# First attention's prologue: bf16 parts taken off in PSUM, rotary in halves, values projected last

## The reference

```python
qkv = jnp.einsum('bnc,dc->bnd', x, W_qkv)
qkv = qkv.reshape(B, N, 6, H, hd).transpose(2, 0, 3, 1, 4)      # H = 16 heads, hd = 8
q = jnp.concatenate((qkv[0], qkv[1]), axis=-1)
k = jnp.concatenate((qkv[2], qkv[3]), axis=-1)
v = jnp.concatenate((qkv[4], qkv[5]), axis=-1)
q = q * cos + rotate_half(q) * sin
k = k * cos + rotate_half(k) * sin
attn1 = jnp.einsum('bhid,bhjd->bhij', q1, k1) * scale
attn2 = jnp.einsum('bhid,bhjd->bhij', q2, k2) * scale
probs = softmax(attn1) - lam * softmax(attn2)
out = einsum('bhij,bhjd->bhid', probs, v)                       # then W_proj
```

## Time and profile before

| | us |
|---|---|
| median of 3 runs | 522.52 |
| lowest and highest | 520.49, 528.23 |
| the profiled execution | 522.95 |
| its span (first to last instruction) | 521.1 |
| PE busy in it | 462.1 (89%) |
| DVE busy in it | 283.0 (54%) |
| DVE's first rotary product to PE's first scores of head 0 | 9.92 to 38.18 |

### The profile page before, as it was taken

One profiled execution on the slowest core, in us unless ns is written; L12 is line 12 of the kernel. 1 busy time (PEld: TensorE's weight loads), 2 busy tenths in 40 slices (PEclk: granted clock), 3 DMA queues, 4 the chain that ended last, 5 costly groups with the idle time before them and its releaser, 6 DMA issues.

```text
span 521.1 us, 10953 instructions
## 1 busy us (share of the span) xinstructions
PE 462.1 (89%) x4143; PEld 333.5 (64%) x4144; DVE 283.0 (54%) x690; ACT 224.5 (43%) x402; POOL 119.1 (23%) x231
## 2 busy tenths in 40 slices
PE   9568999988679998899999597998898999999993
PEld 3424777755445984356767366877795577777773
DVE  2945678724782537554624588988324333332326
ACT  1541677662131424314564246766604543333440
POOL 4821454432300112212211253352200000000001
PEclk9978999999959999989999789999999999999997
DMA  7666454232300001563111000200000011101111
GB/s 179 218 220 150 142 156 153 71 110 86 129 34 1 1 3 32 155 162 103 42 30 40 11 11 18 52 1 0 3 2 11 22 40 40 40 29 32 40 32 41
DMA packets 23020, 34.41 MB, mean 66 GB/s; under 512 B 7568, under 2 KB 15712, under 8 KB 22720
## 3 DMA queue, kind: packets, MB, share of 16 engines
q1 hardware_dynamic: 22976, 33.81, 22.0%
HBM read 28.26 MB, written 5.24 MB: 64 GB/s over the span
## 4 chain that ended last, share of the span: by engine, by line
PE 57%; issue 13%; DVE 12%; DMA 7%; POOL 5%; SPq 2%; ACT 2%; POOLq 0%; DVEq 0%; ACTq 0%
PE ps L1024 11%; PE ps L1007 11%; PE ps L642 4%; PE ps L620 4%; POOL probs L575 4%; PE ps L607 4%; PE ps L995 3%; PE ps L596 2%; PE ps L830 2%; PE ps L864 2%; PE ps L654 2%; DVE arena L1431 2%; DVE arena L1417 2%; DVE bst L1391 2%; PE ps L604 2%
## 5 line engine op out<-in xcount | busy, mean ns | idle before, releaser
L1348 DVE TENSOR_REDUCE negm<-ps 128x4 f32<-128x512 f32 x96 | 64.1, 688 | 43.1 <-PE ps L607 42.0
L1671 DVE SCALAR_TENSOR_TENSOR racc<-ps,sm,racc 128x128 f32<-128x128 f32 x128 | 35.9, 343 | 63.2 <-PE ps L1024 63.1
L1072 ACT ACTIVATE arena<-ps,w1a 128x512 f32<-128x512 f32 x64 | 43.4, 687 | 59.0 <-PE ps L1007 57.8
L1072 ACT ACTIVATE probs<-ps 128x512 f32<-128x512 f32 (+1 forms) x100 | 56.4, 593 | 24.5 <-PE ps L620 23.4
L1024 PEld LDWEIGHTS ps<-w1a,arena 128*128 128x128 f32 x512 | 59.4, 192 | 7.2 <-issue 6.2
L1024 PE MATMUL ps<-w1a,arena 128*128 128x128 f32 x512 | 59.8, 275 | 0.8 <-DVE racc L1662 0.8
L1007 PE MATMUL ps<-xT,w1a 128*128 128x512 f32 x128 | 58.0, 594 | 1.4 <-ACT xT L1072 1.4
L596 PE MATMUL ps<-onesb 128*128 128x512 bf16 x150 | 44.7, 434 | 9.3 <-ACT vall L1072 6.2
L531 POOL TENSOR_SCALAR rstd<-mv 128x4 f32<-128x4 f32 x12 | 2.7, 227 | 182.8 <-DVE mv L1394 182.8
L575 POOL TENSOR_TENSOR probs<-probs,rzE 128x480 f32<-128x480 f32 x32 | 30.6, 987 | 51.7 <-DVE rzE L1613 51.7
L1072 ACT ACTIVATE arena<-ps 128x512 f32<-128x512 f32 (+3 forms) x47 | 26.3, 573 | 32.8 <-PE ps L830 15.4
(11 more groups left out here) (207 smaller groups left out, 826.4 us busy)
## 6 DMA issues: line engine op xcount, KB each, us to landing
stackA<-arena SPq DMA_DIRECT2D x12, 256.0 KB, 2.8
arena<-stackA SPq DMA_DIRECT2D x24, 96.0 KB
arena<-stackA SPq DMA_DIRECT2D x8, 288.0 KB
w1a<-in_w1a SPq DMA_DIRECT2D x1, 2048.0 KB, 8.4
w2a<-in_w2a SPq DMA_DIRECT2D x1, 2048.0 KB, 7.7
w1a<-in_w1b SPq DMA_DIRECT2D x16, 128.0 KB, 2.0
w1a<-in_w2b SPq DMA_DIRECT2D x16, 128.0 KB, 2.0
stackD<-arena SPq DMA_DIRECT2D x6, 256.0 KB
```

Source lines behind the costliest of these rows:

```text
L1072: return nc.scalar.activation(o, i, f, **kw)
L1348: nc.vector.tensor_reduce(negm[:, slot % 2, 4 * g:4 * g + 4], tiles(bank(BANK_S + g % 2), 4, P), AX.X, ALU.max, negate=True).then_inc(a.ma ...
L1671: last = stt(racc[:, b, :], bank(banks + half)[:, k * P:(k + 1) * P], sm[:, 11, bass.ds(b * E1 + e, 1)], racc[:, b, :], ALU.mult, ALU.add)
```

## The change

Only the prologue of the first attention is changed, and the order of the loads.

- DVE's rotary works in four turns: (queries, first half of the tokens), (queries, second half), (keys, first half), (keys, second half). A turn is four products of 512 columns from PSUM into `rope`, a wait for them, and two sums of 512 columns, which DVE now makes itself and **writes back into the two PSUM banks** the operands came from (`A.full`). POOL's four sums are gone.
- ACT rounds from PSUM (512 columns) to part 0. PE then **subtracts** it in PSUM: a bf16 matmul of 512 columns with a stationary minus identity (`minusb`), accumulating on what lies in the bank (`take_off`). ACT rounds the rest to part 1, PE takes it off, ACT rounds to part 2. So DVE's eight instructions of the split are gone, ACT has 24 of 512 columns in place of 8 of 1024, and PE has 16 more matmuls.
- PE makes the projections in the order of the turns; the values come behind the last `take_off`, then the context's keys and values behind `A.lo` 8, and 10 dummy matmuls in place of 26.
- `con` is loaded in three DMAs in place of one: the queries' tables third in the order, ahead of the second half of `xT`; the identity; the rest. `xT`'s first half goes ahead of `wqk0`. `ld_x` now counts `wv0` too.
- SP keeps the parts of n = 0 and 1 when their second half is done, then those of n = 2 and 3, in the order part 0, 1, 2.

```diff
+            load(xT[:, 0:HALF], d["xT"][:, 0:HALF], ld_a)
             load(wqk0[:], d["wqk0"], ld_a)
-            load(xT[:, 0:HALF], d["xT"][:, 0:HALF], ld_a)
+            load(con[:, C_COSQ:C_COSK], d["con"][:, C_COSQ:C_COSK], ld_t)
             load(xT[:, HALF:T], d["xT"][:, HALF:T], ld_h)
-            load(con[:, 0:C_IOTA], d["con"][:, 0:C_IOTA], ld_c)
-            load(wv0[:], d["wv0"], ld_b)
+            load(con[:, 0:C_COSQ], d["con"][:, 0:C_COSQ], ld_c)
+            load(con[:, C_COSK:C_IOTA], d["con"][:, C_COSK:C_IOTA], ld_c)
+            load(wv0[:], d["wv0"], ld_x)
...
-                sp.wait_ge((a.hi, a.mid, a.lo)[p], n + 1)
+                sp.wait_ge((a.hi, a.mid, a.lo)[p], n + 1 if a is D else n // 2 * 4 + n % 2 + 3)
...
-            for n, p in ((0, 0), (1, 0), (0, 1), (2, 0), (1, 1), (0, 2), (3, 0), (2, 1), (1, 2), (3, 1), (2, 2), (3, 2)):
+            for n, p in ((2 * k + m, p) for k in range(2) for p in range(PARTS) for m in range(2)):
...
-            for n in range(4):
-                pool.wait_ge(A.mul, n + 1)
-                op = ALU.subtract if n % 2 == 0 else ALU.add
-                nc.gpsimd.tensor_tensor(rope[:, 2 * n, :], rope[:, 2 * n, :], rope[:, 2 * n + 1, :], op).then_inc(A.full, 1)
-            pool.wait_ge(A.lo, 4)
+            pool.wait_ge(A.full, 8)
             nc.gpsimd.memset(ones_deep, ONES_PAIR).then_inc(zeros, 1)
...
+            def take_off(p, turn):
+                side, half = divmod(turn, 2)
+                for m in range(2):
+                    n = 2 * side + m
+                    pe.wait_ge((A.hi, A.mid)[p], 2 * turn + m + 1)
+                    mm(bank(2 * n + half), minusb[:], part[:, n, p, half * HALF:(half + 1) * HALF],
+                       start=False, stop=True, skip_group_check=True).then_inc((A.rest, A.rest2)[p], 1)
...
+            pe.wait_ge(tables, 5)
+            for turn in range(4):
+                take_off(0, turn)
+                take_off(1, turn)
+            pe.wait_ge(ld_x, 16 * 8)
+            pe.wait_ge(A.lo, 4)
+            first_values(0)
+            first_values(1)
+            first_values(2)
+            first_values(3)
+            pe.wait_ge(A.lo, 8)
...
-            keep_busy(26, BANK_M0)
+            keep_busy(10, BANK_M0)
...
+            for turn in range(4):
+                side, half = divmod(turn, 2)
+                for p, ready, made in ((0, A.full, A.hi), (1, A.rest, A.mid), (2, A.rest2, A.lo)):
+                    for m in range(2):
+                        n = 2 * side + m
+                        act.wait_ge(ready, 2 * turn + m + 1)
+                        fn(part[:, n, p, half * HALF:(half + 1) * HALF], bank(2 * n + half), ACT.Copy).then_inc(made, 1)
...
+            def rotary(side, half):
+                cos, sin = ((C_COSQ, C_SINQ), (C_COSK, C_SINK))[side]
+                dve.wait_ge(A.qk, 2 * side + half + 1)
+                first, second = 2 * side, 2 * side + 1
+                cols = slice(half * HALF, (half + 1) * HALF)
+                for n, other in ((first, second), (second, first)):
+                    for k, (t, table) in enumerate(((n, cos), (other, sin))):
+                        dch(tt(rope[:, 2 * n + k, cols].rearrange("p (a b) -> p a b", b=P),
+                               tiles(bank(2 * t + half), 4, P), over(con[:, table:table + P], 4), ALU.mult))
+                dch.wait()
+                for n, op in ((first, ALU.subtract), (second, ALU.add)):
+                    tt(bank(2 * n + half), rope[:, 2 * n, cols], rope[:, 2 * n + 1, cols], op).then_inc(A.full, 1)
...
-            rotate(0)
-            rotate(1)
-            rotate(2)
-            rest_part(A, 0)
-            rotate(3)
-            rest_part(A, 1)
-            low_part(A, 0)
-            rest_part(A, 2)
-            low_part(A, 1)
-            rest_part(A, 3)
-            low_part(A, 2)
-            low_part(A, 3)
+            dve.wait_ge(ld_t, 16)
+            rotary(0, 0)
+            rotary(0, 1)
+            dve.wait_ge(ld_c, 32)
+            rotary(1, 0)
+            rotary(1, 1)
```

More of the change, by code:

```diff
@@ L116, in decoder_kernel @@
         con = sb("con", [P, C_ALL])
-        identb, trib, onesb, causS, causT = (sb(n, [P, P], BF16) for n in ("identb", "trib", "onesb", "causS", "causT"))
+        identb, trib, onesb, causS, causT, minusb = (
+            sb(n, [P, P], BF16) for n in ("identb", "trib", "onesb", "causS", "causT", "minusb"))
         one = sb("one", [P, 1])
@@ L250, in along @@
             return ap.unsqueeze(2).to_broadcast([ap.shape[0], ap.shape[1], n])
-        ld_a, ld_h, ld_b, ld_c, ld_l, ld_x, ld_r, ld_f, ld_d = (sem(f"ld_{n}") for n in "ahbclxrfd")
+        ld_a, ld_h, ld_c, ld_l, ld_x, ld_r, ld_f, ld_d = (sem(f"ld_{n}") for n in "ahclxrfd")
         zeros = sem("zeros")
@@ L256, in decoder_kernel @@
         tables = sem("tables")
+        ld_t = sem("ld_t")
         dchain, achain, pchain = sem("dchain"), sem("achain"), sem("pchain")
@@ L265, in __init__ @@
                 self.qk = sem(n + "_qk")
-                self.mul = sem(n + "_mul") if turns == 0 else None
+                self.rest2 = sem(n + "_rest2") if turns == 0 else None
                 self.full = sem(n + "_full")
@@ L543, in _ @@
             rsqrt(0, 1)
-            pool.wait_ge(ld_x, 16 * 7)
+            pool.wait_ge(ld_x, 16 * 8)
             add_bias(1, bvB)
@@ L746, in _, with first_values @@
             pe.wait_ge(ld_a, 32)
-            for t in range(4):
+            for side in range(2):
                 for half in range(2):
-                    if t == 0 and half == 1:
+                    if half == 1 and side == 0:
                         pe.wait_ge(ld_h, 16)
[L751 to L756, removed]
+                    for t in (2 * side, 2 * side + 1):
+                        last = mm(bank(2 * t + half), wqk0[:, t, :], xT[:, half * HALF:(half + 1) * HALF],
+                                  start=True, stop=True)
+                    last.then_inc(A.qk, 1)
+            def take_off(p, turn):
[5 more added lines that the diff above has]
+                       start=False, stop=True, skip_group_check=True).then_inc((A.rest, A.rest2)[p], 1)
+            def first_values(g):
                 for k in range(2):
@@ L760, in _ @@
                 last.then_inc(A.vps, 1)
-            pe.wait_ge(ld_x, 16 * 7)
-            pe.wait_ge(A.mul, 4)
+            pe.wait_ge(tables, 5)
[9 more added lines that the diff above has]
+            pe.wait_ge(A.lo, 8)
             for half in range(2):
@@ L773, in _ @@
             pe.wait_ge(fixed, 8)
-            keep_busy(26, BANK_M0)
+            keep_busy(10, BANK_M0)
             pe.wait_ge(bkvc, 4)
             pe.wait_ge(fixed, 8)
-            pe.wait_ge(tables, 4)
             heads(A, NH, pair=False, causal=False)
@@ L1140, in table_of @@
                 ach.wait()
-            act.wait_ge(ld_c, 16)
+            act.wait_ge(ld_c, 32)
+            fn(minusb[:], ident, ACT.Copy, scale=-1.0).then_inc(tables, 1)
             for dst, c in ((identb, C_ID), (trib, C_TRI), (causS, C_CS), (causT, C_CT)):
@@ L1148, in values @@
                 fn(vall[:, 2 * g:2 * g + 2, :], bank(g).rearrange("p (a b) -> p a b", a=2), ACT.Copy).then_inc(A.vall, 1)
-            part_hi(A, 0, rope[:, 0, :])
-            part_hi(A, 1, rope[:, 2, :])
-            part_mid(A, 0, rope[:, 1, :])
+            for turn in range(4):
[5 more added lines that the diff above has]
+                        fn(part[:, n, p, half * HALF:(half + 1) * HALF], bank(2 * n + half), ACT.Copy).then_inc(made, 1)
             values(0)
             values(1)
[L1155 to L1159, removed]
             values(2)
@@ L1431, in low_part @@
                 tt(part[:, n, 2, :], rope[:, 2 * n + 1, :], part[:, n, 1, :], ALU.subtract).then_inc(a.lo, 1)
-            def rotate(n):
-                dve.wait_ge(A.qk, 2 if n < 2 else 4)
-                rotary(n, 0 if n < 2 else 4, *((C_COSQ, C_SINQ) if n < 2 else (C_COSK, C_SINK)))
-            rotate(0)
-            rotate(1)
-            rotate(2)
-            rest_part(A, 0)
-            rotate(3)
-            rest_part(A, 1)
-            low_part(A, 0)
-            rest_part(A, 2)
-            low_part(A, 1)
-            rest_part(A, 3)
-            low_part(A, 2)
-            low_part(A, 3)
+            dve.wait_ge(ld_t, 16)
[4 more added lines that the diff above has]
+            rotary(1, 1)
             dve.wait_ge(ld_l, 16 * 6)
```

## The result

| | us |
|---|---|
| changed kernel, median of 20 runs | 520.94 (518.83 to 527.01) |
| kernel before, median of 20 runs | 524.67 (520.49 to 542.69) |
| ratio | 0.994, interval 0.9917 to 0.9963 |
| the profiled execution of the changed kernel, and its span | 521.54, 519.4 |

The changed kernel is faster by 0.6%, some 3.1 us (1.9 to 4.4), less than the 2% that count as a change here. The ratio leaves out the executions that ran at a lower granted clock, so it isn't the quotient of the two medians. The forecast of 517.6 was a gain of 4.9 on 522.52, the median of three runs of the kernel before. Twenty give 524.67. So of the 3.3 us between forecast and result, 2.15 are this start, and about 1.2 (4.9 less 524.67 - 520.94 = 3.7) the gain itself.

A forecast was written before the change was run, and what follows sets the result against it. It took DVE's rotary and split, then write landings and head stacks, to bound the prologue. 3.65 + 1.25 = 4.9 us off 522.95 gave 518.05, less 0.4 to the median: 517.6, range 514 to 521.8.

The forecast's parts named there:

- DVE bounds the prologue, and the split's subtractions are what to take off it: Prologue: DVE on the chain without a gap from 9.92 to 30.64 us, the split's last subtraction at 28.29.
- DVE starts at 7.7; a turn is 3.75; last sum at 22.8: Rotary on DVE: start after two projection matmuls instead of four, then four turns of products and sums.
- The sums' price, 0.60 apart: DVE's sums into PSUM, which no row priced: 0.60 us taken, 1.7 as upper bound; each 0.1 more costs 0.8.
- DVE paces, ACT has slack: Rotary turns: ACT needs 3.0 to 3.5 us a turn, less than DVE's 3.75.
- Last part at 25.8, writes landed at 28.5, 4.3 us earlier: End of the split: last rounding at 25.8 instead of 30.64, plus 2.1 and 0.6 for the writes to land.
- The queue of writes: Last parts' writes: six of 256 KB released within 3 us, so 0.6 us added to the landing.
- PE's values at 25.3, at half clock until 28.8; heads from 36.4: PE behind the last subtraction: values until 30.7, context's projections until 34.3, 10 dummies, then heads; head 2 reached at 42.5.
- The thin stretch: PE during the turns: 16 matmuls of 0.2 to 0.4 us in 12 us, which should bring the half clock.
- The dip behind this wait: Half clock behind PE's wait for head 2's stack, expected to go with the 1.9 us stall, worth 1.25 us.
- 3.65 + 1.25 = 4.9 at head 1: Heads: PE reaches head 2 at 42.5 instead of 46.15, 3.65 us earlier, and the vanished half clock gives 1.25.
- Nothing behind that is changed: Rest of the kernel: code unchanged, so the whole 4.9 us comes off the profiled 522.95, giving 518.05.
- The rival "more": No half clock at 25, no queued writes, 6.3 us gained: 516.3; later dips may differ by a us or two; chance 0.15.

The follow-up runs named there:

- five profiles: Profiles with the old prologue's DVE work: kernel before, its repeat, twice with 40 more dummy matmuls, once with new load order; stack loads issued at 31.53 to 32.82 us.
- the second pair: Kernel before and changed kernel, both run again unchanged: ratios 1.0002 and 0.9897 to the kernel before, spans 522.7 and 516.9 us.
- the second profile: The changed kernel run again unchanged: ratio 0.9897 to the kernel before, span 516.9 us, head 1 at 47.95.
- The first pair: First profiles of the kernel before and the changed kernel: spans 521.1 and 519.4 us; ratio 0.994.
- The four comparisons: Changed kernel against kernel before: first run, repeat, and both kernels with 40 more dummy matmuls, twice; 3.1, 5.4, 5.0 and 4.3 us faster.
- the nine profiles of the table: Kernel before twice, with new loads, with sums on DVE; changed twice, with 26 dummies, values earlier, DVE held; 467.6 to 471.2 us behind head 1.
- the 40 dummies: 40 more dummy matmuls in PE's waits behind the first attention: ratios 0.9943, 0.9944 on the kernel before; 0.9847, 0.9862 on the changed kernel.

## Why the prediction was right or wrong

- *DVE bounds the prologue, and the split's subtractions are what to take off it.* The first half is shown: the stack loads followed DVE's first product by 22.9 us in five profiles, and the sums alone on DVE made head 1 4.2 us later. Of the 4.8 us at the stack loads some 2.4 came with the subtractions, the sums and the halves together, and the rest goes with the earlier start; what the subtractions alone are worth isn't shown.
- *DVE starts at 7.7; a turn is 3.75; last sum at 22.8.* It started at 7.20, a turn was 3.72 (7.20, 10.93, 14.65, 18.37), the last sum ended at 22.18. Right. Starts differ by over a microsecond from run to run in both kernels, which I had not allowed for.
- *The sums' price, 0.60 apart.* 0.696 us long, 0.60 apart. Right. The 120 cycles against 58 of the Trainium skill (VectorE: DVE Perf Modes, "The TRN2 errata") are for results in SBUF, and the difference isn't seen here either: the sums, which read SBUF (and write PSUM), took 15 ns more than the products, which read PSUM, and not some 65 less, as an estimate from these two figures would have it.
- *DVE paces, ACT has slack.* Only half right. The chain lies on ACT and PE from 12.2 on. ACT's last turn took 3.6 us (eight roundings without a gap in 4.81), where 3.0 to 3.5 was expected, so nothing is left below a start of 7.5.
- *Last part at 25.8, writes landed at 28.5, 4.3 us earlier.* 25.41 and 27.97, 4.8 earlier. The queue of writes that I allowed 0.6 for cost about 0.4 (2.5 us from the last rounding's end to the landing).
- *PE's values at 25.3, at half clock until 28.8; heads from 36.4.* The thin stretch did bring the half clock (0.50 from 16.8 us on). Values from 24.57, and 4.36 us for all of them instead of 5.4, as the clock was full again at about 26. Heads from 34.29. Too dear by 2 us, and that is why `w1a` (expected 41.8, came at 41.5) and not PE was the later, contrary to my sum; PE still waited 1.2 us there. The dip behind this wait did stay away.
- *3.65 + 1.25 = 4.9 at head 1.* Measured 5.26 and, of the second pair, 5.25. The direction and the sum are right up to here, but the two terms were off in opposite ways, which is luck: head 2's scores came 4.6 us earlier (46.15 to 41.57), and from there to head 1 only 0.7 were gained. The row of maxima that took 5.11 us behind the stacks' transfers wasn't in the sum and cost PE 0.6, and 1.0 in the second profile.
- *"Nothing behind that is changed", so 4.9 reach the end: 522.95 - 4.9 = 518.05, and 517.6.* This is the step that failed. The code is the same, but its time isn't: 467.6 to 471.2 us, with the half clock and late rows of maxima where the profiles differ. I subtracted from one execution, which by the table was the best of nine behind head 1, and from a median of three, 2.15 us under that of twenty. The first pair was 5.26 us apart at head 1 and 1.7 at the end. The four comparisons give 3.1, 5.4, 5.0 and 4.3 us, 4.5 in the mean, so the size of the gain was nearly right, and its absolute time and what one comparison would show of it were not.
- The range of 514 to 521.8 held 520.94, and "within 2%" came. The rival "more" had the right remark, that later dips may fall differently by a us or two; it belonged in the forecast, not in a rival.

**What stays open.** In the nine profiles of the table, behind head 1, the kernels like before took 469.1 in the mean of four, those like the changed one 470.0 in the mean of five. PE's waits for the rows of maxima (`arena<-mT`, 56 to 115 us) were 1.2, 1.1, 0.5 and 1.3 us in the four and 2.9, 1.3, 1.9, 1.3 and 2.2 in the five. With the 40 dummies the rest took 465.3 and 466.3 like before, and 466.0, 470.5 and 466.9 changed. So some 0.9 us of the gain, or more, may be given back systematically, by waits for transfers that come later behind the stacks'. With this spread it isn't shown, and no experiment here separates it. Why the clock falls in one execution and not in the next is open too.

## What to carry to other kernels

Split work between engines by who holds the chain: subtracting with a minus identity in PSUM took eight instructions off the bound engine, for 16 matmuls on an engine that had slack. With the sums, the work in halves and an earlier start it was worth 5.3 us where the chain left the prologue, and about 2 of these were the start. Don't put work of 3 us into a thin stretch of an engine whose next small instruction is on the chain. And when a gain is 1%, take the level behind it from several profiles: code that isn't touched moved by 3.6 us.

## What the runs showed of the hardware

- A VectorE `tensor_tensor` of 512 columns from SBUF into PSUM took 0.696 us, one with an operand in PSUM and the result in SBUF 0.681.
- In this kernel TensorE matmuls (16, L764) accumulate on what VectorE wrote into PSUM, where matmuls had filled the same banks before.
- The half clock at one place of the same code came in six of nine profiles, and these were 2 us longer in the mean behind head 1. In the Trainium skill (TensorE: Matmul & The Clock Gate, "Why this matters for your kernels") long pauses between bursts of matmuls are named as what brings it; the trace differs: the half clock at 125.1 came behind two short pauses, of 1.05 and 0.92 us, around a group of four transposes. Nor do the pauses decide it: the same two, to 0.01 us, stand in the kernel before and in the changed kernel's second profile, where the clock stayed full.
- The same prologue's first VectorE product came between 8.64 and 9.92 us. In two of its four profiles a load ended last ahead of it or of its matmuls (half of `xT`, the table), in the other two TensorE's matmuls.
- A transfer of 12 KB behind those of the stacks took 5.11 and 4.44 us to land, and 2.3 us later on.
